# A state-space layer with experts on one core: the seventh inflow product of each unit goes from VectorE to GpSimd, from a copy of B

## The reference

```
state = exp(delta * A) * state + delta * u * B[t]
y     = sum over the 16 states of state * C[t]
```

## Time and profile before

| | |
|---|---|
| median of 3 runs | 861.06 us (860.25 to 862.83) |
| profiled execution | 859.91 us, its span 858.1 us |
| busy: VectorE, TensorE, GpSimd, ScalarE | 691.1, 628.7, 530.0, 423.3 us |
| mean granted clock of TensorE | 0.87 |

### The profile page before, as it was taken

How to read it: one execution, slowest core, us unless ns; L and a number is a source line. 1 busy time by engine, 2 the same in 40 slices (tenths; PEclk the granted TensorE clock), 3 DMA queues, 4 the chain that set the end, 5 groups by cost and what they waited for, 6 DMA issues and landing times. The chain is left out here.

```text
span 858.1 us, 12506 instructions
## 1 busy us (share of the span) xinstructions
PE 628.7 (73%) x3035; PEld 298.0 (35%) x3035; DVE 691.1 (81%) x1353; ACT 423.3 (49%) x884; POOL 530.0 (62%) x526
## 2 busy tenths in 40 slices
PE   3777788888887887888888757567315999898920
PEld 2221222222322222222222122122114888888810
DVE  3067799999999999999898999999531777776754
ACT  4526658368376555647537634234012554454524
POOL 5215566756787768769578768768761555454433
PEclk9877989999999999999799887697655999999965
DMA  3065446567479675656546656662013665666646
GB/s 85 0 172 132 113 110 160 119 164 163 95 175 234 132 184 123 147 135 154 118 103 170 143 124 158 138 145 65 22 58 104 175 175 171 177 174 169 175 136 174
DMA packets 60390, 117.39 MB, mean 137 GB/s; under 512 B 8816, under 2 KB 37296, under 8 KB 52256
## 3 DMA queue, kind: packets, MB, share of 16 engines
q1 hardware_dynamic: 56000, 107.60, 51.5%
q0 software_dynamic: 4320, 8.99, 3.3%
HBM read 100.21 MB, written 16.35 MB: 136 GB/s over the span
## 5 line engine op out<-in xcount | busy, mean ns | idle before, releaser
L535 POOL TENSOR_TENSOR hc<-hs,Crep 128x1024 f32<-128x1024 f32 x128 | 301.1, 2356 | 155.4 <-DVE hs L1312 129.8
L1312 DVE TENSOR_TENSOR_SCAN hs<-bank,state,flow 128x512 f32<-128x512 f32 x256 | 313.6, 1267 | 23.1 <-ACT bank L1076 17.3
L1076 ACT ACTIVATE bank<-bank,negA 128x512 f32<-128x512 f32 x256 | 164.3, 659 | 234.4 <-PE bank L755 234.2
L755 PE MATMUL bank<-delta,sel 64*128 64x512 f32 x512 | 166.6, 731 | 95.0 <-DVE hs L1312 94.9
L1302 DVE TENSOR_TENSOR flow<-flow,bank 128x2048 f32<-128x2048 f32 x63 | 142.8, 2266 | 0.7 <-PE bank L743 0.7
L1203 ACT ACTIVATE flow<-bank,b1T 128x128 f32<-128x128 f32 x284 | 80.9, 368 | 80.1 <-PE bank L941 80.1
L755 PEld LDWEIGHTS bank<-delta,sel 64*128 64x128 f32 x512 | 44.4, 210 | 192.4 <-DVE hs L1312 152.1
L941 PE MATMUL bank<-flow 128*128 128x128 f32 x568 | 83.0, 291 | 13.8 <-issue 7.9
L645 POOL DMA_INDIRECT results<-flow,idn x71 | 69.8, 983 | 33.3 <-issue 33.3
L764 PE MATMUL bank<-hc,kc 128*32 128x512 f32 x512 | 74.5, 656 | 10.5 <-POOL hc L535 10.5
L941 PEld LDWEIGHTS bank<-flow 128*128 128x128 f32 x568 | 71.2, 197 | 26.8 <-issue 15.8
(11 more groups left out here) (185 smaller groups left out, 769.4 us busy)
## 6 DMA issues: line engine op xcount, KB each, us to landing
flow<-du_d SPq DMA_DIRECT2D x63, 1024.0 KB, 7.1
flow<-L_ffn_W SPq DMA_DIRECT2D x71, 256.0 KB
xg<-xs SPq DMA_DIRECT2D x71, 66.0 KB
hs<-results SPq DMA_DIRECT2D x16, 256.0 KB, 4.6
du_d<-du SPq DMA_DIRECT2D x28, 128.0 KB, 3.0
xin<-L_attn_x SPq DMA_DIRECT2D x8, 256.0 KB, 3.4
out<-hc SPq DMA_DIRECT2D x8, 256.0 KB, 2.6
results<-flow,idn POOLq DMA_INDIRECT x71
```

The source lines that it names most:

```text
L535: nc.gpsimd.tensor_tensor(hc[:, Q % 2, two, :], hs[:, Q % 2, two, :], Crep[u % 3][:].unsqueeze(1).broadcast_to([P, 2, T]), ALU.mult).then_ ...
L755: ins = nc.tensor.matmul(dbank[2 * odd + i][:], sel[rows, odd, q % 4, :], delta[u % 2][rows, q // 4, :])
L1076: nc.scalar.activation(dbank[G % 4][:], dbank[G % 4][:], ACT.Exp, scale=negA[:, ch:ch + 1]).then_inc(s_ex, 1)
L1312: nc.vector.tensor_tensor_scan(hs[:, Q % 2, j, :], dbank[G % 4][:], flow[Q % 3][:, j, :], state[:, Q // QUADS % 2, Q % QUADS, j:j + 1], AL ...
```

## The change

The inflow product of the seventh quad of each unit (`LENT = 6`) is made by GpSimd. As GpSimd can't read the bank `Brep`, ScalarE copies B to SBUF once a unit, `B_sb`, at its step 1, as soon as VectorE's product of the unit's first quad is done (`copy_b`). GpSimd makes the quad's product in two halves, 128x1024 each: one behind slot 10, one behind slot 11 (`lent_inflow`). VectorE leaves this product out, and the first scan of the quad waits for both halves. VectorE's second inflow product of a unit waits for the copy. The pairs of row lists go from slots 10, 11, 13 and 14 to slots 7, 12, 13 and 14. The counts of the waits on inflow products follow.

```diff
+LENT = 6
+        B_sb = sb("B_sb", [P, T])
+        def by_dve(Q):
+            return sum(q % QUADS != LENT for q in range(Q + 1))
@@ store_du (SyncE)
-                after(sp, s_bu, QUADS * (u - 1))
+                after(sp, s_bu, by_dve(QUADS * (u - 1) - 1))
+                after(sp, s_bp, 2 * (u - 1))
@@ GpSimd
+            def lent_inflow(u, half):
+                Q = QUADS * u + LENT
+                if half == 0:
+                    pool.wait_ge(s_bc, u + 1)
+                    pool.wait_ge(s_dul[Q % 3], 16 * (Q // 3 + (Q % 3 != 0)))
+                part = flow[Q % 3][:, 2 * half:2 * half + 2, :]
+                nc.gpsimd.tensor_tensor(part, part, B_sb[:].unsqueeze(1).broadcast_to([P, 2, T]), ALU.mult)\
+                    .then_inc(s_bp, 1)
@@ host(j) of GpSimd, behind times_c of the slot
+                    if slot in (10, 11):
+                        lent_inflow(j, slot - 10)
-                        if slot in (10, 11, 13, 14):
-                            first_row = 2 * (10, 11, 13, 14).index(slot)
+                        if slot in (7, 12, 13, 14):
+                            first_row = 2 * (7, 12, 13, 14).index(slot)
@@ spread_b (TensorE)
-                after(pe, s_bu, QUADS * u)
+                after(pe, s_bu, by_dve(QUADS * u - 1))
+                after(pe, s_bc, u)
@@ ScalarE
+            def copy_b(u):
+                act.wait_ge(s_bu, by_dve(QUADS * u))
+                after(act, s_bp, 2 * u)
+                nc.scalar.copy(B_sb[:], Brep[:]).then_inc(s_bc, 1)
@@ host(j) of ScalarE, behind decay of the step
+                    if g == 1:
+                        copy_b(j)
@@ inflow(Q) of VectorE
+                if q == LENT:
+                    return
+                if q == 1:
+                    dve.wait_ge(s_bc, u + 1)
@@ scan(G) of VectorE
                 if G % 4 == 0:
-                    dve.wait_ge(s_bu, Q + 1)
+                    if Q % QUADS == LENT:
+                        dve.wait_ge(s_bp, 2 * (Q // QUADS) + 2)
+                    else:
+                        dve.wait_ge(s_bu, by_dve(Q))
```

More of the change, by code:

```diff
@@ L278, in mamba_moe @@
         s_ex = sem("decay_done")
-        s_bu = sem("inflow_done")
+        s_bu = sem("inflow_done_by_dve")
+        s_bp = sem("inflow_done_by_pool")
+        s_bc = sem("B_copied")
         s_sc = sem("scan_done")
```

## The result

The changed kernel takes 892.86 us (median; 890.89 to 897.89) against 860.65 us of the kernel before in the same comparison: 1.038 times as long, 95% interval 1.033 to 1.043, some 33 us slower. The forecast was 884 us, range 874 to 901. The profiled execution is the longest of the changed kernel's (897.89 us, span 896.1), so it is compared by stages: its eight units, from the first scan to the end of the last product with C, take 587.6 us (57.1 to 644.7) against 554.2 (57.3 to 611.5). That is 33.4 us, and is what is explained here. The remaining 4.8 us lie behind them: the expert stage and the final sums take 251.4 us against 246.6, and between 249.3 and 253.2 in the profiled executions of the experiments, with no relation to their edits. The other three executions of the changed kernel are 4 to 7 us shorter than the profiled one.

A forecast was written before the change was run, and what follows sets the result against it. VectorE was taken to set the pace in the eight-unit stage. Terms 28.4 - 7.5 + 4.6 - 8.9 + 0.6 + 6 = +23.2 us on 859.91 gave 883.1; with the median 1.15 higher, 884 was forecast, range 874 to 901.

The forecast's parts named there:

- rival 2: The stall comes with heavy clock losses, or `oh` meets slot 15's product again: 890 to 902 us; chance 0.22.
- The stall: Before scan 24, VectorE waits for GpSimd's second half: 3.12 us in units 0 to 4, 4.28 in 5 to 7; +28.4 us.
- The giveback: VectorE's idle time before scan 27, waiting for ScalarE's Silu, vanishes: 1.05 us in units 0 to 4, 2.22 in 5; -7.5 us.
- TensorE's clock: Idle 4.6 us around scan 25, TensorE drops to 1.2 GHz, delaying later decays: 1 us in six units, +6 (0 to 18).
- One-hots: `oh`, held beside slot 15's product in units 3, 4, 5 and 7, moves clear of it: 4 x -2.2 = -8.9 us.
- the copy: ScalarE's copy of B delays decays 2 and 3: about 0.9 us in units 1 to 5, +4.6 us; other end 0.
- I take it as escaped: Assumes `oh` comes 16.6 us after scan 24, at slot 14's product's tail or beside the lists; -8.9 us.
- The lists and the tail: Two lists at slot 7 are free; the last unit's end after slot 15 grows 4.9 us against 4.3: +0.6 us.
- GpSimd's load as such: Rival tested in the experiments: GpSimd's added work itself slows the stage, by contention or total; the prediction said its total doesn't enter.
- Contention beside the lent halves: Claimed no VectorE instruction inside GpSimd's four products is held, so the stall term stays; only `oh` moves.

## Why the prediction was right, point by point

The direction, the range and the main mechanism came true. The single number was too low: the 892.86 us lie outside the band of 877 to 890 us to which I gave 0.60, and in that of rival 2, which had 0.22 and tells what happened: heavier losses over the clock, and one-hots that meet slot 15's product again.

- **The stall (28.4 us forecast).** Measured 28.0 us in quad 5. Scan 24 came 9.35 to 9.37 us after slot 10's start in all units, forecast 9.42. Two more lists in the chain made it 12.1 to 12.3, and with a reader one quad later the stall was gone and scan 24 came after 6.31 and 5.14 us, as before the change. The cause is shown.
- **The giveback (-7.5).** Measured -6.9: 1.15 in units 1 to 4, 2.32 in unit 5, none in unit 0, whose Silu stands at another step.
- **TensorE's clock (+6, between 0 and 18).** Mechanism right, and shown by keeping TensorE busy. The size was 9.5 us. I had taken 1 us in each of six units; in units 1 to 5 it is nothing where the clock is back within 7 us of scan 24, and 1.7 to 3.1 where it takes 11 to 14. The expected idle stretch of 4.6 us measured 4.54. For the same reason the scans' waits for ScalarE, which I expected to fall by 7 us, are 19.2 us against 17.3: quad 7 adds what quad 6 gives back.
- **One-hots (-8.9) and the copy (+4.6).** Together I had -4.3; quad 0 measured +3.1. This is the step that failed: "I take it as escaped". It has two reasons. The reckoning was that of an undisturbed unit, while the text two paragraphs on lets the same unit lose 1 to 3 us to the clock; that loss carries scan 0 from the gap of the lists into slot 15's product (units 3 and 5). It stood among the rivals, with nearly the right condition (a loss of 2.3 to 5 us; 2.0 was enough in unit 4, 1.7 was not in unit 1), but not in the sum. And units 5 and 6 have no `front_rstd`, so GpSimd's products come 2 us earlier behind them: the one-hots of units 6 and 7 meet slot 15's product even with TensorE kept busy and quad 7 at 8.25 us in all of units 1 to 6 (3.00 us both). The copy itself was overpriced: 0.6 us in each of units 1 and 2, hidden elsewhere. It was luck that this error went against the other and made the miss smaller.
- **The lists and the tail (+0.6).** The last unit's end, from scan 24 to the end of slot 15's product, is 19.4 us against 19.0. The experiment without the lent product shows no clean price for the move of two lists to slot 7: its ratio is 1.0048, that of the copy alone 1.0041.
- **The rivals.** GpSimd's load as such was not what cost: with the eighth quad it carries the same 37.6 us, and the kernel gains 1.2%. Contention beside the lent halves was judged right for the chosen slots and the seventh quad, and only for them: at slots 8 and 9 it takes most of the gain of quad 5 (0.4 us left of 2 in unit 5), and it shows in unit 0 with the eighth quad.

The sum was 23 us for 33: 7.4 us too little in quad 0, 3.5 in quad 7, and under 1 elsewhere. The range held because these two were its open ends.

## What to carry to other kernels

When work moves to an engine that is less busy, ask for the time between the moment when its input can be ready in that engine's own order, and the moment when its reader needs the result; the engine's total says nothing about it. If the stretch is too short, look for another piece of the same work with a later reader before looking for an earlier slot: here one quad later turned +3.8% into -1.2%. And carry each loss on through the sum: what one term delays is the starting time of the next. Where a small instruction is held by a large one of another engine, look at the one behind it as well before calling it free.

## What the runs showed of the hardware

A stall of the leading engine can cost twice. Behind each idle stretch of TensorE of 4.5 us at this place (units 1 to 5) the granted clock was 0.50 for 6.8 to 13.7 us in the changed kernel, and four spreading products took 2.08 us, not 1.13.

VectorE instructions with two SBUF inputs (`oh`; `taken` behind it; the product of delta and u) were held beside GpSimd's products, and the last one held a product itself. Scans (1.25 to 1.29 us), gates (0.66 to 0.68) and inflow products (at most 2.29), which read a PSUM bank and one SBUF tile of data, kept their times in all runs. The Trainium skill (SBUF — State Buffer, Who interferes with whom) says that a VectorE instruction with two SBUF inputs contends with a GpSimd instruction that reads SBUF; the trace agrees.

What surprised me is when the hold begins. A held `oh` ends 0.09 us behind the product, a held `taken` 0.06, but many of them started ahead of it by the profile. In the changed kernel one-hots started at 424.36 and the product at 424.91, and they were held all the same, for 3.00 us, longer than the product of 2.36; the largest lead of a held instruction is 0.67 us (`taken`, 3.08 us, with the Silu at step 25). At step 2, with 0.54 us left of one product, `oh` was held through the next as well, whereas the product of delta and u, which asked 2.1 us before the end of a product, got in between two. A fixed lead doesn't explain it: with one-hots at step 30 two `taken` with leads of 0.41 and 0.53 us ran free (0.19 us), and the `oh` above with 0.03. Four one-hots of the last unit, 0.18 to 0.19 us ahead of a product, seem to run free as well, but the hold only falls on the second instruction. In the changed kernel it is:

```profile
637.35 0.20 DVE L1388 TENSOR_TENSOR oh<-kc,topi 128x64 f32<-128x64 f32 x1
637.58 2.37 DVE L1394 TENSOR_TENSOR taken<-oh 128x32 bf16<-128x32 f32 x1
```

```profile
637.54 2.35 POOL L543 TENSOR_TENSOR hc<-hs,Crep 128x1024 f32<-128x1024 f32 x1
```

So the recorded starts alone don't tell who goes first, and what decides it is open.
